# Attention stage of a one-core kernel: when inside a sequence the next projections, the rows of maxima and the preceding output are issued

## The reference

```python
xn = layer_norm(x, in_ln_w, in_ln_b)
proj = xn @ W_in.T + b_in                    # q, k, v, p of 256 each, y of 16
# k is smeared with the key before it, by a factor of each head;
# the gate of y gives a running sum over positions that is added to the scores
attn = softmax(causal scores of 16 heads of 16 features)
o = attn @ v
out = silu(p) * o @ W_out.T
return layer_norm(out, out_ln_w, out_ln_b)
```

## Time and profile before

| | before |
|---|---|
| median of 3 runs | 1752.04 us (1747.55 to 1752.73) |
| profiled execution, its time | 1751.51 us |
| its span | 1749.8 us |
| PE busy | 1393.7 us (80%) |
| DVE busy | 1195.0 us (68%) |
| ACT busy | 695.5 us (40%) |
| POOL busy | 412.0 us (24%) |
| mean granted clock of PE | 0.662 of full |

### The profile page before, as it was taken

The page is one execution under the profiler, slowest core; times in us unless marked ns, Lnnn a source line. Parts: engine busy times, 40 slices in busy tenths (PEclk is TensorE's granted clock), DMA queues, the critical chain, the costliest instruction groups (busy, mean ns, idle before and its releaser), DMA issues. The chain is left out here.

```text
span 1749.8 us, 65439 instructions
## 1 busy us (share of the span) xinstructions
PE 1393.7 (80%) x27355; PEld 1028.1 (59%) x27370; DVE 1195.0 (68%) x5759; ACT 695.5 (40%) x2428; POOL 412.0 (24%) x700
## 2 busy tenths in 40 slices
PE   5788888888888888888888863598989889879576
PEld 4677777777767777677777742255555454445333
DVE  5667777777777777777777755477767767747265
ACT  3333232222222222222222211166656656657465
POOL 2011111111111111111211125333144244201344
PEclk6555555555555555555555556699999999989789
DMA  5200000000000000000000002946375375370001
GB/s 116 24 4 5 6 5 4 6 17 7 5 6 6 5 19 5 7 5 5 18 5 7 5 6 51 134 78 81 49 99 74 47 107 70 44 93 1 1 13 37
DMA packets 68363, 55.77 MB, mean 32 GB/s; under 512 B 11086, under 2 KB 67302, under 8 KB 68070
## 3 DMA queue, kind: packets, MB, share of 16 engines
q1 hardware_dynamic: 65894, 51.41, 19.5%
q10 hardware_dynamic: 2176, 0.20, 0.1%
HBM read 33.93 MB, written 17.56 MB: 29 GB/s over the span
## 5 line engine op out<-in xcount | busy, mean ns | idle before, releaser
L716 PE MATMUL PS<-GB,W 128*128 128x8 f16 x18432 | 575.8, 168 | 180.2 <-DVE GB L1026 174.5
L716 PEld LDWEIGHTS PS<-GB,W 128*128 128x128 f16 x18432 | 532.6, 104 | 288.9 <-DVE GB L1026 282.5
L1926 DVE TENSOR_REDUCE MX<-PS 128x1 f32<-128x512 f32 (+3 forms) x352 | 223.3, 637 | 162.5 <-PE PS L1651 159.9
L920 ACT ACTIVATE tr<-PS 128x16 f32<-128x16 f32 x512 | 93.7, 183 | 491.3 <-PE PS L716 491.3
L1807 ACT ACTIVATE PT<-PS 128x512 f32<-128x512 f32 (+1 forms) x352 | 194.3, 559 | 167.4 <-PE PS L1667 165.1
L1012 DVE SCALAR_TENSOR_TENSOR u_<-tr,PS 128x16 f32<-128x16 f32 x512 | 87.8, 171 | 126.3 <-PE PS L716 114.5
L922 ACT ACTIVATE tz<-PS 128x16 f32<-128x16 f32 x512 | 93.7, 183 | 194.6 <-PE PS L716 194.6
L1648 PE MATMUL PS<-KS,QS 99*128 99x256 bf16 (+3 forms) x512 | 135.4, 317 | 30.5 <-issue 10.3
L670 POOL TENSOR_TENSOR rt<-mv,eps 128x1 f32<-128x1 f32 x96 | 18.4, 192 | 553.8 <-DVE mv L1037 553.8
L1019 DVE SCALAR_TENSOR_TENSOR zg<-tz,HR 128x16 f32<-128x16 f32 x512 | 90.1, 176 | 81.0 <-ACT tz L922 80.9
L729 PE MATMUL PS<-Y,V 128*128 128x32 f16 x2322 | 130.9, 188 | 0.0
(11 more groups left out here) (363 smaller groups left out, 2524.3 us busy)
## 6 DMA issues: line engine op xcount, KB each, us to landing
QS<-q_parts SPq DMA_DIRECT2D x48, 256.0 KB
KS<-k_parts SPq DMA_DIRECT2D x48, 256.0 KB
q_parts<-PQ SPq DMA_DIRECT2D x16, 384.0 KB, 12.5
k_parts<-PK SPq DMA_DIRECT2D x16, 384.0 KB, 14.3
x_steps<-XM SPq DMA_DIRECT2D x32, 64.0 KB, 1.5
out_dram<-X SPq DMA_DIRECT2D x8, 256.0 KB, 2.3
X<-x_steps SPq DMA_DIRECT2D x4, 448.0 KB
XM<-in_L_attn_x_dram SPq DMA_DIRECT2D x16, 80.0 KB
```

Source lines behind the costliest of these rows:

```text
L716: return pe.matmul(bank[:, p, at:at + B], W[:, kc, w:w + P], state[:, part, kc, :], start=False, stop=True, skip_group_check=True)
L920: act.activation(as_states(tr), now(pR), ACT.Tanh, scale=gate_scale).then_inc(hn_tr.sem, 1)
L1926: dve.tensor_reduce(MX[:, g % 2, heads[0]:heads[-1] + 1, NT - 1 - it], p_x[:, k % 2, 0:len(heads) * w].rearrange("p (a w) -> p a w", w=w), ...
```

## The change

Every step keeps its operands, its waits and its place within a slot. What changes is the slot: `project_qk` is 1 to 3 slots later on all engines (its first normalisation, in slots 0 and 1, stays), `project_v` 5 slots later, `output` from 4 slots later at its start to none at its end (POOL's L1554 stays in slot 10). The transposes of the maxima (L1677) go from the 7th to the 8th of the 11 slots, behind a multiplication by the values, and ACT's four copies L1796, which were one a slot in slots 7 to 10, are now one in 8, one in 9 and two in 10. The diff in full, without context:

```diff
@@ -1537 +1537 @@
-                    for c in {6: (0,), 8: (1,), 12: (2,), 14: (3,)}.get(i, ()):
+                    for c in {8: (0,), 10: (1,), 14: (2,), 16: (3,)}.get(i, ()):
@@ -1555 +1555 @@
-                    if i == 28:
+                    if i == 32:
@@ -1557 +1557 @@
-                    if i == 33:
+                    if i == 36:
@@ -1562 +1562 @@
-                    if i == 39:
+                    if i == 40:
@@ -1576 +1576 @@
-                    if i == 2:
+                    if i == 3:
@@ -1583 +1583 @@
-                    if i == 4:
+                    if i == 6:
@@ -1591 +1591 @@
-                    for c in {4: (0,), 6: (1,), 7: (2,), 8: (3,)}.get(i, ()):
+                    for c in {6: (0,), 8: (1,), 9: (2,), 10: (3,)}.get(i, ()):
@@ -1598 +1598 @@
-                    for t in {10: (0, 1), 11: (2,), 12: (3,)}.get(i, ()):
+                    for t in {12: (0, 1), 13: (2,), 14: (3,)}.get(i, ()):
@@ -1610 +1610 @@
-                    if i == 18:
+                    if i == 21:
@@ -1619 +1619 @@
-                    for t in {24: (0,), 26: (1,), 28: (2,), 30: (3,)}.get(i, ()):
+                    for t in {29: (0,), 31: (1,), 33: (2,), 35: (3,)}.get(i, ()):
@@ -1672 +1672 @@
-                    if k == 6:
+                    if k == 7:
@@ -1729 +1729 @@
-                    for c in {17: (1,), 20: (0,)}.get(i, ()):
+                    for c in {21: (1,), 24: (0,)}.get(i, ()):
@@ -1745 +1745 @@
-                    for half in {22: (0,), 23: (1,)}.get(i, ()):
+                    for half in {26: (0,), 27: (1,)}.get(i, ()):
@@ -1766 +1766 @@
-                    if i == 3:
+                    if i == 4:
@@ -1769 +1769 @@
-                    for c in {5: (0,), 7: (1,), 8: (2,), 9: (3,)}.get(i, ()):
+                    for c in {7: (0,), 9: (1,), 10: (2,), 11: (3,)}.get(i, ()):
@@ -1778 +1778 @@
-                    if i == 6:
+                    if i == 8:
@@ -1781 +1781 @@
-                    if i == 19:
+                    if i == 22:
@@ -1788 +1788 @@
-                    for t in {25: (0,), 27: (1,), 29: (2,), 31: (3,)}.get(i, ()):
+                    for t in {30: (0,), 32: (1,), 34: (2,), 36: (3,)}.get(i, ()):
@@ -1793,2 +1793 @@
-                    if k >= 7:
-                        i = k - 7
+                    for i in {8: (0,), 9: (1,), 10: (2, 3)}.get(k, ()):
@@ -1817 +1816 @@
-                    for c in {18: (1,), 21: (0,)}.get(i, ()):
+                    for c in {22: (1,), 25: (0,)}.get(i, ()):
@@ -1820 +1819 @@
-                    if i == 24:
+                    if i == 28:
@@ -1873 +1872 @@
-                    if i == 5:
+                    if i == 7:
@@ -1877 +1876 @@
-                    if i == 7:
+                    if i == 9:
@@ -1880 +1879 @@
-                    for c in {9: (0,), 11: (1,)}.get(i, ()):
+                    for c in {11: (0,), 13: (1,)}.get(i, ()):
@@ -1883 +1882 @@
-                    for c in {10: (0,), 12: (1,)}.get(i, ()):
+                    for c in {12: (0,), 14: (1,)}.get(i, ()):
@@ -1888 +1887 @@
-                    if b == 0 and i == 13:
+                    if b == 0 and i == 15:
@@ -1890,2 +1889,2 @@
-                    if 17 <= i < 17 + NT and b + 1 < B:
-                        if i == 17:
+                    if 20 <= i < 20 + NT and b + 1 < B:
+                        if i == 20:
@@ -1895,2 +1894,2 @@
-                        moments(b + 1, i - 17)
-                    if i == 22 and b + 1 < B:
+                        moments(b + 1, i - 20)
+                    if i == 24 and b + 1 < B:
@@ -1898 +1897 @@
-                    if i == 14:
+                    if i == 17:
@@ -1901 +1900 @@
-                    if i == 15:
+                    if i == 18:
@@ -1904 +1903 @@
-                    if i == 16:
+                    if i == 19:
@@ -1917 +1916 @@
-                    for t in {26: (0,), 28: (1,), 30: (2,), 32: (3,)}.get(i, ()):
+                    for t in {31: (0,), 33: (1,), 35: (2,), 37: (3,)}.get(i, ()):
@@ -1987 +1986 @@
-                    if i == 25:
+                    if i == 29:
@@ -1990 +1989 @@
-                    if i == 26:
+                    if i == 30:
@@ -1992,2 +1990,0 @@
-                    if i == 27:
-                        aggregate(0, b)
@@ -1994,0 +1992,2 @@
+                        aggregate(0, b)
+                    if i == 34:
@@ -1996 +1995 @@
-                    if i == 32:
+                    if i == 35:
@@ -1998 +1997 @@
-                    if i == 37:
+                    if i == 38:
@@ -2001,2 +1999,0 @@
-                    if i == 38:
-                        stats(1, N1, b, (2, 3))
@@ -2003,0 +2001,2 @@
+                        stats(1, N1, b, (2, 3))
+                    if i == 40:
```

More of the change, by code:

```diff
@@ L1986, in output @@
                 def output(b, p, i):
-                    if i == 25:
+                    if i == 29:
                         dve.wait_ge(t_kept.sem, t_kept.value(dve, b))
                         stats(0, T, b, (0, 1))
-                    if i == 26:
+                    if i == 30:
                         stats(0, T, b, (2, 3))
-                    if i == 27:
+                    if i == 31:
                         aggregate(0, b)
-                    if i == 31:
+                    if i == 34:
                         normal(0, N1, T, b, (0, 1), n1)
-                    if i == 32:
+                    if i == 35:
                         normal(0, N1, T, b, (2, 3), n1)
-                    if i == 37:
+                    if i == 38:
                         dve.wait_ge(n1w.sem, n1w.value(dve, b))
                         stats(1, N1, b, (0, 1))
-                    if i == 38:
+                    if i == 39:
                         stats(1, N1, b, (2, 3))
-                    if i == 39:
+                    if i == 40:
                         aggregate(1, b)
```

## The result

| | before | changed |
|---|---|---|
| median, 18 runs each | 1749.11 us | 1741.75 us |
| all runs | 1746.93 to 1756.17 | 1733.92 to 1752.62 |
| ratio of the two | | 0.995 (95%: 0.9935 to 0.9965) |
| span of the profiled execution | 1749.8 us | 1743.4 us |

The changed kernel is faster by 7.4 us by the medians, 8.7 by the ratio; -16 was forecast, from 1751.5 to 1736. Its median lies in the range given. Its own runs spread over 19 us, those of before over 9: that turns out to be part of the explanation.

What follows compares the result with a forecast made beforehand. Limits change within a pass: PE's waits, DVE in slots 11 to 14 and 33 to 40, stack transfers needing 34.1 us. Passes -18, body 0 -2, body 7 -1.6, ACT +6 gave -16: 1736 us, range 1724 to 1756.

Steps and rivals of the forecast that it cites:

- The cap by the stacks: Ahead of slot 22, stack transfers allow -3.4 us a pass of -4.7; a KS wait of about 1 us appears.
- XN, XT, L1677, L1742: First half waits gone: XN -0.8, XT -0.56, two L1677 -1.1, L1742 for KA -1.15, KAT -0.47, second L1742 -0.5 us.
- with the waits gone I take the clock to stay up: First half: TensorE's half clock ahead of slot 22 goes, about 1.5 us a pass comes back.
- Wrong: half clock moved behind slot 22: Sign that the forecast fails: half clock in the second half, up to 1.5 us a pass.
- KK, +1.4 in slots 11 to 14: Two KK steps, 0.51 and 1.23 us, enter slots 11 and 12 where DVE is the limit; KA's 0.36 leaves slot 14.
- Second half, -0.2: Slots 22 to 43: L1742 +0.5, L1750 -0.34, one L1677 -0.55, work moved into slots 33 to 40 +0.2 us.
- ACT's pair, +6: Two copies directly ahead of the next group's exponentials pass on 0.2 us a group, some 30 groups; range 0 to +18.
- the stacks are no limit: Rival: transfers run shorter or ACT's pair costs nothing, first half gains its whole 4.7 us; 1725 us, chance 0.13.
- A wash: Rival: waits only change their place, slots 11 to 14 and 33 to 36 being full; 1748 us (1743 to 1758), chance 0.27.
- DVE and POOL hold each other up: Rival: KK and QA steps held by POOL, slots 11 to 14 over 10 us; 1773 us, chance 0.10.

Runs made afterwards that it cites:

- the early write: Loop's k parts written to DRAM before SP waits for the end of the body: changed kernel 1722.47 us (0.9852), kernel before 1748.99 us (1.0005).
- the uncapped kernel: Changed kernel with k's parts written early and the stacks read 8 heads at a time: 1708.85 us, ratio 0.977.
- the two experiments: Apparently L1677 and its copies put back in the kernel with stacks read 8 heads at a time, 1708.87 us, and moved alone on the kernel before, 1749.52 us.
- halves: Stacks read 8 heads at a time, k's parts written early: changed kernel 1708.85 us (0.977), kernel before 1733.05 us (0.9908).
- the KK steps moved out: KK moved to slots 15 to 18 in the changed kernel with k's parts written early: 1718.38 us (0.9821); with stacks also read 8 heads at a time: 1698.03 us.
- The kernel with halves and KK moved: Changed kernel, k's parts written early, stacks read 8 heads at a time, KK steps in slots 15 to 18: 1698.03 us, ratio 0.9711.

## Why the prediction came out as it did

The sum was -16; the ratio says -8.7. By its own steps:

- **The cap by the stacks, -3.4 a pass instead of -4.7.** Right, and the main point: without it the early write would have gained nothing in the passes. The five first halves won 15.8 us where -17 stood. That the sum fits so well is in part luck, as only three of the five waited some 2 us for the stacks and one was as long from half clock alone. The wait for KS in these is 1.96 to 2.63 us where "about 1 us" stood, since the first half uncapped is shorter than worked out: 31.5 against 37.1 is -5.6, not -4.7.
- **XN, XT, L1677, L1742.** The waits went as forecast. Slots 0 to 3 take 4.4 instead of 5.1 us (-0.8 forecast), slots 4 to 10 take 12.2 instead of 13.5 (-1.1 for XT and one L1677), slots 15 to 21 take 9.7 instead of 12.9 with the stacks out of the way: -3.2, where the terms for one L1677, KA, KAT, the second L1742 and the half clock made -4.2 and the debt of KK (below) +1.0. For L1677 by itself the term of -0.55 was wrong in the first half, where undoing it in the uncapped kernel changes nothing. In the second it was near in size (0.4 and 0.5 a pass in the two experiments), but in the uncapped kernel it came in slots 33 to 40, where the forecast gave it nothing.
- **Half clock: "with the waits gone I take the clock to stay up".** This is the step that failed. I named a wait of 1 us in slot 22 and did not follow it to the clock, though the earlier trace rows showed what such a wait does. In three of five passes the clock fell in the second half, for 3.4 to 10 us, and cost 9.1 us in the profiled execution, 5.9 of it behind the wait for stacks; with early writes or halves those second halves are 29.7 us. In the first half, too, it did not stay up: it fell in three of five passes, behind the waits for maxima that had taken the place of those for KA, and only the cap kept that from showing. "Wrong: half clock moved behind slot 22" was the sign given for it, at up to 1.5 us a pass; it measured up to 4.
- **KK, +1.4 in slots 11 to 14.** In size near (1.0 a pass by the KK steps moved out), in place wrong, for slots 11 to 14 became shorter (5.2 us against 5.65): PE is two items ahead of DVE, so the debt falls due in slot 15.
- **Second half, -0.2.** Without half clock it is 29.7 against 29.5, +0.2. Slots 33 to 40 rose by 2.3 us, near the upper bound of +2.8 by DVE, and slots 26 to 32 by 0.6; slots 22 to 25 fell by 2.7.
- **ACT's pair, +6.** Wrong: 0, the lower bound. I take the reason to be that where the copy is late PE is behind DVE's reductions anyway.

The half clock and the pair of copies are errors of opposite sign, so that the total missed by less than its parts, and that the median lies in the range is luck as far as they cancel. Of the rivals, "the stacks are no limit" is refuted by these waits, in the fifth pass until 34.1 us after the issue; the early write made that case true by another edit, and gave 1722.5 us where the rival stood at 1725 (its five passes add up to -24.5 and not to the -23 written there). "A wash" began 1.3 us above the measured median. Its picture, waits that change their place, is what the waits for maxima show (6.3 us before, 17.9 now), but none of its prices came: the pair of copies cost nothing, slots 11 to 14 became shorter and the undisturbed second half is at +0.2, not +1.3. What brought the time near it is the half clock. "DVE and POOL hold each other up" did not come: slots 11 to 14 took 5.2 us, not over 10, although one KK step shows the hold:

```profile
1350.52 1.65 DVE L1884 SCALAR_TENSOR_TENSOR KK<-KF_,qsc,KK 128x511 f32<-128x511 f32 x1
...
1349.65 0.72 POOL L1531 CAST PQ<-RES 128x512 bf16<-128x512 f32 x1 [0.17 <-POOL RES L1529]
1350.45 1.17 POOL L1533 TENSOR_TENSOR PQ<-RES,PQ 128x512 bf16<-128x512 f32 x1
```

L1884, 0.74 us at its shortest in that pass before the change, began 0.07 us after a POOL instruction and took 1.65 us, 0.55 beyond that instruction's end at 1351.62; in the prediction's row the end of a cast matched the end of a POOL instruction to 0.05 us. The Trainium skill (SBUF — State Buffer, "Who interferes with whom") has one engine wait until the other's instruction is over. The trace fits that for these two, but eight steps did not each pay for one.

The Trainium skill (TensorE: Matmul & The Clock Gate, "HAM oscillation") ties the fall of the clock to longer idle times than these. In the changed kernel a wait of 2.04 us, in the one before of 1.15 us, was followed by half clock, so the measurement goes against it. The kernel with halves and KK moved has no wait of PE longer than 0.64 us in its loop passes, and saw half clock twice there, 3.4 us each: single waits are not the whole rule either, and which it is stays open.

## What to carry to other kernels

When a step leaves the critical path, look for the transfer that has to land by the same point, measured from its issue in a place where nothing else delays its use: here one row, 34.1 us, told within 1 us where the first half would end in each pass that waited for the stacks. Then follow the wait that takes over to what it does to TensorE's clock: the wait itself cost no more than the cap, but passes 2 and 5, with 10.2 us of half clock behind it and in slots 33 to 40, took 68.0 and 67.4 us, longer than before the change (67.7 and 66.5). Take the cap away first, then order the slots: the same tables were worth 7.4 us under the cap and 24.2 us without it, and the best version here, with halves and the k steps later, is at 1698 us, 3% below the kernel before.

## What the runs showed of the hardware

- The granted clock fell to 0.50 behind waits of PE of 1.15 us (before) and of 1.96 to 2.63 us (changed), but also where no wait was longer than 0.97 us (changed, first halves) or 0.64 us (with halves and KK moved, slots 33 to 40). In the changed kernel it fell at other places from one pass to the next, and the runs spread over 19 us; in the one before once a pass at the same place, with a spread of 9.
- Reads of the stacks that follow each other without a pause came with two stalls of PE of 3.7 and 3.8 us for which the trace names no releaser, in the kernel before; the changed kernel with the same early write had none in its loop passes.
